# The short last pair of score chunks comes fifth in its group, and its two PSUM banks also take the transposed maxima of another group

## What is computed

```python
q = layernorm(x)                                   # (4, 256, 128)
qh, kh, vh = split_heads(q), split_heads(ctx), split_heads(ctx)   # 16 heads of 8
scores  = einsum('bhqd,bhkd->bhqk', qh, kh) + mask # 4 x 16 x 256 x 1601
weights = softmax(scores, axis=-1)
out     = einsum('bhqk,bhkd->bhqd', weights, vh)
x = x + relu(out @ wo_w.T + wo_b)
```

## Time and profile before

| | us |
|---|---|
| three runs | 862.52, 863.67, 865.89 (median 863.67) |
| profiled execution | 863.95 |
| its span, first to last instruction | 862.0 |
| mean granted clock of TensorE | 0.922 |
| PE busy | 694.7 (81%) |
| DVE busy | 525.2 (61%) |
| ACT busy | 452.5 (52%) |

### The profile page before, as it was taken

The page is one execution under the profiler, slowest core; times in us unless marked ns, Lnnn a source line. Parts: engine busy times, 40 slices in busy tenths (PEclk is TensorE's granted clock), DMA queues, the critical chain, the costliest instruction groups (busy, mean ns, idle before and its releaser), DMA issues.

```text
span 862.0 us, 13508 instructions
## 1 busy us (share of the span) xinstructions
PE 694.7 (81%) x5026; PEld 340.9 (40%) x5026; DVE 525.2 (61%) x863; ACT 452.5 (52%) x765; POOL 132.6 (15%) x167
## 2 busy tenths in 40 slices
PE   4754684488877538989899889989879999999996
PEld 3443353255545403333333323333235445445544
DVE  3575885388895574888788888888114233333323
ACT  3633483588884106777687677768842221212221
POOL 5155610000000081321240141000000000000000
PEclk8886798699998857999999999999888999999999
DMA  6323659311112002010710520001100110111100
GB/s 191 134 71 112 212 183 203 115 47 54 46 38 77 1 0 77 2 41 19 193 40 2 126 87 2 2 1 45 45 2 1 43 43 13 31 43 43 43 1 24
DMA packets 30647, 52.83 MB, mean 61 GB/s; under 512 B 3838, under 2 KB 23882, under 8 KB 30148
## 3 DMA queue, kind: packets, MB, share of 16 engines
q0 software_dynamic: 3424, 26.23, 11.3%
q1 hardware_dynamic: 27172, 25.89, 9.6%
HBM read 39.71 MB, written 12.00 MB: 60 GB/s over the span
## 4 chain that ended last, share of the span: by engine, by line
PE 55%; DVE 17%; issue 7%; ACT 7%; DMA 7%; SPq 4%; POOL 2%; ACTq 0%; DVEq 0%; POOLq 0%
PE pair L964 13%; PE pair L886 11%; DVE smax L1361 7%; PE pair L861 6%; PE pair L817 5%; PE pair L955 5%; DVE region_p L1273 4%; DMA mask_sb<-in_mask_Bx1xSxS_ff 4%; PE pair L973 4%; SPq L450 3%; ACT region_p L1156 2%; PE pair L690 2%; PE pair L726 2%; DVE region_p L1243 2%; PE pair L792 2%
## 5 line engine op out<-in xcount | busy, mean ns | idle before, releaser
L1361 DVE TENSOR_REDUCE smax<-pair 128x2 f32<-128x1024 f32 x192 | 225.4, 1220 | 52.2 <-PE pair L817 52.0
L1156 ACT ACTIVATE region_p<-pair 128x1024 f32<-128x1024 f32 (+3 forms) x277 | 217.7, 812 | 63.6 <-PE pair L861 58.0
L964 PE MATMUL pair<-region_p,region_g 128*128 128x512 f32 x256 | 118.8, 607 | 2.8 <-DVE region_p L1424 2.6
L1189 ACT ACTIVATE region_p<-pair,bias_T 128x512 f32<-128x512 f32 x32 | 22.0, 687 | 122.8 <-PE pair L964 122.8
L1424 DVE SCALAR_TENSOR_TENSOR region_p<-pair,bias_T,region_p 128x512 f32<-128x512 f32 x32 | 24.0, 751 | 98.2 <-ACT region_p L1189 98.2
L726 PE MATMUL pair<-ident,region_p 128*128 128x128 f32 x256 | 38.2, 297 | 46.0 <-DVE region_p L1276 46.0
L1243 DVE SCALAR_TENSOR_TENSOR region_p<-region_p 128x1024 int16<-128x1024 int16 (+1 forms) x56 | 67.1, 1220 | 10.0 <-ACT region_p L1064 7.4
L964 PEld LDWEIGHTS pair<-region_p,region_g 128*128 128x128 f32 x256 | 46.8, 193 | 62.7 <-issue 55.3
L886 PE MATMUL pair<-region_p 128*32 128x256 f32 (+1 forms) x832 | 67.7, 399 | 0.5 <-ACT region_p L1163 0.4
L886 PE MATMUL pair<-region_p,v_aug 128*32 128x256 f32 (+1 forms) x832 | 66.5, 391 | 0.4 <-ACT region_p L1163 0.4
L817 PE MATMUL pair<-region_k,qstack 56*128 56x512 bf16 (+1 forms) x256 | 44.7, 369 | 22.4 <-DVE smax L1361 13.2
(11 more groups left out here) (172 smaller groups left out, 900.9 us busy)
## 6 DMA issues: line engine op xcount, KB each, us to landing
kimg<-region_k SPq DMA_DIRECT2D x56, 200.1 KB
region_k<-kimg POOLq DMA_DIRECT2D x8, 1400.9 KB, 17.4
mask_sb<-in_mask_Bx1xSxS_ff POOLq DMA_DIRECT2D x12, 800.5 KB, 5.6
region_p<-in_mask_Bx1xSxS_ff POOLq DMA_DIRECT2D x4, 800.5 KB, 13.3
region_g<-in_L_ffn_W SPq DMA_DIRECT2D x24, 128.0 KB, 2.2
region_g<-in_L_ffn_Wg SPq DMA_DIRECT2D x8, 256.0 KB, 2.9
region_g<-in_L_ffn_Wl SPq DMA_DIRECT2D x8, 256.0 KB, 3.0
wnat<-in_L_attn_w_qkv SPq DMA_DIRECT2D x8, 192.0 KB, 4.7
```

The lines of the kernel that those rows point to most:

```text
L964: last = pe.matmul(pair[2][:, n * 512:(n + 1) * 512], w[:, u, f, half * 128:(half + 1) * 128], zed[:, c, f, :], start=(f == 0), stop=(f == 1))
L1156: act.activation(pT[0:rows, first // 3 % 2, k:k + size], home[0:rows, 0:size], ACT.Exp).then_inc(expt_made, 1)
L1361: dve.tensor_reduce(units[:, :, c // 3, c % 3], both, AX.X, ALU.max).then_inc(slot_done, 1)
```

## The change

The pairs of a group are reordered by a table `UNITS`: pair 4 is now the short one, and pairs 5 to 12 are the full ones that were 4 to 11. The maxima of group s no longer have a slot of their own. Their transposition is written into the same slot as the short pair of group s + 1, behind its eight matmuls, in columns of the bank that the rests leave free. VectorE reduces the rests, copies the maxima and signals `slot_done` once. The reduction of `smax` into `nmax` follows the pair that is last in order, now a full one. The maxima of the last group have no short pair beside them and keep a slot of their own, one pair position later than before.

```diff
-SETTLED = 4
+TAIL_AT = 4
+UNITS = tuple(range(TAIL_AT)) + (KT - 1,) + tuple(range(TAIL_AT, KT - 1))
...
-def maxima_after(p):
-
-    s, late = divmod(p - (KT - 1) - SETTLED, KT)
-    return s if late == 0 and 0 <= s < GROUPS else None
+def maxima_with(p):
+
+    s, i = divmod(p - KT, KT)
+    return s if i == TAIL_AT and 0 <= s < GROUPS else None
...
     def pair_of_chunks(p):
-        if p < PAIRS:
+        if p < PAIRS or maxima_with(p) is not None:
             order.append(("chunks", p))
-        if maxima_after(p) is not None:
-            order.append(("maxima", maxima_after(p)))
...
-    return {key: n for n, key in enumerate(order)}
+    table = {key: n for n, key in enumerate(order)}
+    for s in range(GROUPS):
+        table["maxima", s] = table["chunks", KT * (s + 1) + TAIL_AT]
+    return table
...
-QUERIES_AT = KT + SETTLED - 1
+QUERIES_AT = KT + TAIL_AT - 1
+MAXIMA_AT = 4 * REST // 2 * 2 + 60
...
                     for r in range(4):
                         for a in range(2):
                             last = one(a, r, r * REST, 3 * CHUNK, REST)
+                    if maxima_with(p) is not None:
+                        last = maxima_T(s - 1, home)
                 last.then_inc(slot_full, 1)

-            def maxima_T(s):
-
-                n = SLOT["maxima", s]
+            def maxima_T(s, home):
+
                 pe.wait_ge(nparts_made, s + 1)
-                wait(pe, slot_done, n - 1)
-                pe.transpose(pair[n % 2][:, :].bitcast(BF16)[0:24, 0:128], nparts[:, s % 2, :], identb[:, :]).then_inc(slot_full, 1)
+                return pe.transpose(maxima_in(home), nparts[:, s % 2, :], identb[:, :])
...
                 if c < KT - 1:
-                    dve.tensor_reduce(units[:, :, c // 3, c % 3], both, AX.X, ALU.max).then_inc(slot_done, 1)
+                    last = dve.tensor_reduce(units[:, :, c // 3, c % 3], both, AX.X, ALU.max)
                 else:
-                    dve.tensor_reduce(units[:, :, :, 3], both[:, :, 0:4 * REST].rearrange("p a (r k) -> p a r k", r=4),
-                                      AX.X, ALU.max).then_inc(slot_done, 1)
+                    last = dve.tensor_reduce(units[:, :, :, 3], both[:, :, 0:4 * REST].rearrange("p a (r k) -> p a r k", r=4),
+                                             AX.X, ALU.max)
+                    if maxima_with(p) is not None:
+                        last = maxima_move(s - 1, pair[n % 2])
+                last.then_inc(slot_done, 1)
+                if p % KT == KT - 1:
                     dve.wait_ge(slot_done, n + 1)
                     wait(dve, nparts_made, s - 1)
                     dve.tensor_reduce(nmax[:, s % 2, :], smax[:, s % 2, :, :], AX.X, ALU.max, negate=True).then_inc(nmax_made, 1)
```

More of the change, by code:

```diff
@@ L110, in slot_table @@
     order += [("finish", B - 1, piece) for piece in range(3)]
-    return {key: n for n, key in enumerate(order)}
+    table = {key: n for n, key in enumerate(order)}
+    for s in range(GROUPS):
+        table["maxima", s] = table["chunks", KT * (s + 1) + TAIL_AT]
+    return table
 SLOT = slot_table()
-QUERIES_AT = KT + SETTLED - 1
+QUERIES_AT = KT + TAIL_AT - 1
+MAXIMA_AT = 4 * REST // 2 * 2 + 60
+assert MAXIMA_AT + 64 <= CHUNK
 X2_AT = event_of(2 * (KT * (GROUPS - 2) + KT - 2))
@@ L299, in decoder_layer, with maxima_in @@
         st_bank = (pair[2][:, 0:512], pair[2][:, 512:1024], pair[3][:, 0:512])
+        def maxima_in(home):
+            return home[:, :].bitcast(BF16)[0:24, 2 * MAXIMA_AT:2 * MAXIMA_AT + 128]
         def qkv_home(hp, c):
@@ L803, in chunks @@
             def chunks(p, masked):
-                n, (s, c), home = SLOT["chunks", p], divmod(p, KT), pair[SLOT["chunks", p] % 2]
+                n, s, c, home = SLOT["chunks", p], p // KT, UNITS[p % KT], pair[SLOT["chunks", p] % 2]
                 b, g = divmod(s, HG)
@@ L842, in pair_of_chunks @@
                     chunks(p, masked)
-                if maxima_after(p) is not None:
-                    maxima_T(maxima_after(p))
+                elif maxima_with(p) is not None:
+                    wait(pe, slot_done, SLOT["chunks", p] - 1)
+                    maxima_T(maxima_with(p), pair[SLOT["chunks", p] % 2]).then_inc(slot_full, 1)
             def tile_scores(e, masked):
@@ L1352, in chunk_maxima @@
             def chunk_maxima(p):
-                n, (s, c) = SLOT["chunks", p], divmod(p, KT)
+                n, s, c = SLOT["chunks", p], p // KT, UNITS[p % KT]
                 if c == 0:
@@ L1367, in chunk_maxima, with maxima_move @@
                     dve.tensor_reduce(nmax[:, s % 2, :], smax[:, s % 2, :, :], AX.X, ALU.max, negate=True).then_inc(nmax_made, 1)
-            def maxima_move(s):
-                n = SLOT["maxima", s]
+            def maxima_move(s, home):
                 wait(dve, shift_loaded, 32 * (s - 1))
-                dve.wait_ge(slot_full, n + 1)
-                dve.tensor_copy(nmT[:, s % 2, :], pair[n % 2][:, :].bitcast(BF16)[0:24, 0:128]).then_inc(slot_done, 1)
+                return dve.tensor_copy(nmT[:, s % 2, :], maxima_in(home))
             def pair_of_chunks(p):
@@ L1378, in pair_of_chunks @@
                     chunk_maxima(p)
-                if maxima_after(p) is not None:
-                    maxima_move(maxima_after(p))
+                elif maxima_with(p) is not None:
+                    dve.wait_ge(slot_full, SLOT["chunks", p] + 1)
+                    maxima_move(maxima_with(p), pair[SLOT["chunks", p] % 2]).then_inc(slot_done, 1)
             def finish_tiles(b, piece, home):
```

## The result

The changed kernel takes 860.57 us (median of 20 runs) against 866.36 for the kernel before (20 runs, among them the three shown above). The ratio is 0.9935, with a 95% interval of 0.9909 to 0.9961. "No change" was forecast and it is faster by 0.65%, so the forecast was wrong. The time itself lies in the range of 857.0 to 868.5. The profiled execution took 862.17 us, its span is 860.4 us and the mean granted clock 0.923.

What follows compares the result with a forecast made beforehand. Neither engine saturated: TensorE and VectorE wait on a two-slot ring, then on the maxima's DMAs. Groups +1.4, group 13 +0.3, lead -1.45 give +0.25 us: 863.9 us median, range 857 to 868.5, "no change" 72%.

Steps and rivals of the forecast that it cites:

- The ring: Score stage, two slots between TensorE and VectorE: the maxima's own slot costs 1.11 to 1.14 us, removed by the change.
- The three classes: Groups 1, 4, 7, 10; 2, 8, 11, 14; 3, 6, 12, by slot place: 0.0, +0.4, -0.1 us per group.
- The wait behind it: A group's first score tile waits for two DMAs of copied maxima, taken as 3.07 us after the copy ends.
- the eleven groups: Groups 1 to 14 without 5, 9 and 13, waiting for the maxima's DMAs: together +1.4 us.
- Group 13: Its finish piece would wait for a full reduction instead of the short one: +0.3 us.
- (a): Rival: DMA of the maxima is no bound, gain as meant, below 859.4 us; 854.4 at 2.2 us latency; 15%.
- Groups 5 and 9: They already wait for the end of a burst of loads, which a later copy hardly moves: 0 us.
- Lead: Ahead of the score stage: query transposes come first, no longer behind group 0's transposition waiting for GpSimd: -1.45 us.
- (b): Rival: the DMA wait more than eats the gain; at 3.66 us latency +6.5 us, near 870; 8%.
- (c): Rival: the clock falls in TensorE's new waits, four times 3.5 us, near 878 us; 5%.
- (d): Rival: the change does not remove the wait in the ring of slots; given no share of its own.

Runs made afterwards that it cites:

- late_masks_after: Changed kernel with GpSimd's mask loads of batches 2 and 3 and their two mask_clamp steps one group later; 860.86 us, ratio 0.993.
- late masks: Mask loads and mask_clamp steps one group later, in the kernel before (863.25 us, ratio 0.9965) and the changed kernel (860.86 us, 0.993).
- reorder_only: Kernel before with the short pair fifth in its group, the maxima still in a slot of their own; 864.95 us, ratio 0.9989.
- TAIL_AT = 3: Changed kernel with the short pair fourth in its group, so the shared slot comes one pair earlier; 857.88 us, ratio 0.9906.
- TAIL_AT = 4: The changed kernel itself, short pair fifth in its group, against the kernel before; 860.57 us, ratio 0.9935.

## Why the prediction was wrong

**The ring: right.** The slot of the maxima cost 1.11 to 1.14 us, and its waits vanished. The three classes, the place of each shared slot and who waits behind it came out as written.

**The wait behind it: the step that failed.** I set the transfer at 2.2 + 0.87 = 3.07 us. The 2.2 us to the last packet come from a quiet stretch, the 0.87 us from the last packet to TensorE from group 5, in the middle of a load. The two do not belong together. In a quiet stretch the sum is 2.67, so from packet to engine it takes 2.67 - 2.2 = about 0.5. In the words of the prediction 0.87 was "nearest", because it was measured on this transfer; it was measured under the one condition that the eleven groups of the sum don't share. The mechanism was right and its size was off by 0.40. In late_masks_after, where the loads do not stand ahead of it, group 9 itself has 2.69. With 2.67 in the same lines:

| class | forecast cost | with 2.67 | measured | measured cycles |
|---|---|---|---|---|
| group 1 | 0.91 | 0.51 | 0.49 | 3.88 and 4.07 against 3.73 |
| group 2 | 1.53 | 1.13 | 1.14 | 4.87 against 3.73 |
| group 3 | 0.93 | 0.53 | 0.49 | 4.46 against 3.97 |

(354.75 - 350.87 = 3.88, 358.82 - 354.75 = 4.07, 375.52 - 370.65 = 4.87, 395.15 - 390.69 = 4.46; 3.97 is the same cycle, 389.21 to 393.18, before.) The waits themselves were up to 0.3 us shorter than 2.67 gives, in part since the shared slot takes 0.39 us of TensorE (352.58 to 352.97) rather than 0.28 and the tile is wanted a little later. The cost is the same. The sum over the eleven groups is then 4 (-0.39) + 4 (-0.01) + 3 (-0.47) = -3.0 us, where I had +1.4. Group 13 has the same transfer in it, which I left out both here and in rival (a), so its +0.3 becomes -0.1. Together that is -3.1 us instead of +1.7: this term alone is 4.8 us, over half a per cent, and turns "no change" into "faster".

By the Trainium skill, "DMA: Bandwidth & Descriptors", section "Anatomy of one DMA — SWDGE (gpsimd) path", the estimate in the prediction, from its fixed cost of about 2.0 us, was 2.75 us. The 2.67 measured here agrees with it better than with my own value, although the page writes of the other issue path.

**Groups 5 and 9: right for the wait, wrong for what followed.** I put them at 0, since a later copy would hardly move the end of a burst. From the first tile of group 4 to that of group 5 it took 21.39 us before and 21.28 after, from group 8 to group 9 23.02 and 22.93: the 0 held. But behind the wait of 1.94 us in group 9 (1.01 before) the clock fell. From its tile to that of group 10 it took 17.93 us (504.76 to 522.69), against 16.83 in late_masks_after, whose clock stays at 1.00: 1.1 us, for which the sum had no term. So the stage comes to -3.1 - 0.2 + 1.1 = -2.2 us, and -2.5 was measured.

The late masks take both waits and the low clock away on both sides. Then all of groups 1 to 14 follow the three classes, and the same arithmetic gives 5 (-0.39) + 5 (-0.01) + 4 (-0.47) + 0.3 = -3.6 us, the 0.3 for the finish piece. Measured: 269.15 - 272.12 = -3.0. That this is near is in part luck, since two misses of the arithmetic stand against each other. In an undisturbed round of three groups, from the tile of group 1 to that of group 4, the changed kernel gained 1.3 us (407.22 - 354.18 = 53.04 before, 408.80 - 357.05 = 51.75 after) and not 0.87: the cycle ahead of the slot of group 3 became 0.36 shorter as well (380.22 to 384.37 before, 383.17 to 386.96 after). And from group 4 to group 5, where the first batch is finished, it lost 0.84 us with late masks (20.15 and 20.99). Neither has a term in the prediction.

**Group 13: right in kind.** Its finish piece, on TensorE of the changed kernel, waits 0.53 us longer than the earlier trace rows, as forecast:

```profile
568.34 0.43 PE L914 MATMUL pair<-ident,region_p 128*128 128x128 f32 x2 [0.89 <-DVE smax L1370]
```

**Lead: near in size, doubtful in cause.** Forecast -1.45, measured -0.7 to -1.4 us without the burst. That the transposes come first explains it in the kernel before and not in the changed one, and the short pair among the last five, worth 0.6 to 1.0 us in reorder_only, was not in the sum.

**The rivals.** (a) was nearest: its point of decision, "below a latency of 2.8 us", was passed, but not by far, so a third of its gain came. That point was itself misplaced: 863.9 less 0.4 in each of eleven groups is 859.5 us, so by the same sum the total leaves "no change" only at some 2.66 us, and with the 2.75 it is 860.4 and still inside. A shift of 0.4 us was all that it took, and 15% for what lies behind it was too little. (b) falls. (c) happened in group 9, as a cost of 1.1 us rather than 3.5, and not in the groups that wait 1.08 us. (d) falls as well, since the waits of the ring are gone.

**Balance.** Stage -2.5, lead -0.7 to -1.4, together 3.2 to 3.9 us of the 5.8 between the medians. Between 1.9 and 2.6 us are not accounted for; the interval of the ratio itself reaches from 3.4 to 7.9 us. The rest of the span differs by 2.4 us in the two profiles, but it varies by 6 us among kernels with the same code there, so I don't claim them for the change.

## What to carry to other kernels

When a stall goes, size the next wait from rows taken under the same load: a duration made of one part from a quiet stretch and another from a busy one fits neither. Before a small transfer is shortened, look at what else stands in the DMA queues when it is issued: moving a large load behind the small one that is awaited was worth 2.3 to 5.7 us of the stage here for a few moved lines, while a second queue for the small one lost 3.9 and 8.4. (In the whole time of late_masks_after the gain did not show.) And where two orders differ by one position, cost the neighbouring positions too. TAIL_AT = 3 gives the transfer 3.0 to 3.3 us of room instead of 1.6 to 2.5 (the 2.67 less the waits of 1.08 to 0.19) and was worth 6.6 us of stage more than TAIL_AT = 4.

## What the hardware showed that was not expected

Waits of one to two microseconds on TensorE amid dense work were sometimes followed by the low granted clock (0.50) and sometimes not. It fell during, or within 2.2 us behind, waits of 1.24, 1.58, 1.88, 1.93, 1.94, 2.10, 2.14, 2.18, 2.90, 3.32 and 3.60 us, for 3 to 14 us each time. It did not behind 1.01, 1.12, 1.17, 1.27, 1.29, 1.38 and 1.41 us, nor anywhere in the stage of the kernel before. The two groups overlap, so the length of the wait alone does not decide it. Where it fell for 3.4 us it cost 1.1 us of the stage, where for 7 us 2.6, so the wait of 1.88 us cost 4.50 us in all, more than twice its length.

A small DMA issued by GpSimd (L630, 0.62 us of issue) while GpSimd's own loads were under way reached TensorE 4.2 us after its issue; in a quiet stretch it took 1.8 us.
